# One unit's way through a cross-attention kernel, spread over three slots

## What is computed

```
res = x
h = _layer_norm(x, ln1_scale, ln1_offset)
x = res + _cross_attention(h, xf_1, wq1, bq1, wk1, bk1, wv1, bv1, wo1, bo1, bias_k1, bias_v1)
...
h = _layer_norm(x, ln_mlp_scale, ln_mlp_offset)
h = jax.nn.gelu(h @ w_fc1 + b_fc1, approximate=False) @ w_fc2 + b_fc2
return x + h
```

```
logits = jnp.einsum('bqhk,bthk->bhqt', qh, kh) / scale
weights = jax.nn.softmax(logits, axis=-1)
ctx = jnp.einsum('bhqt,bthk->bqhk', weights, vh).reshape(b, q_len, H * K)
return ctx @ wo + bo
```

## Time and profile before

| what | us |
|---|---|
| median of 3 runs | 1518.13 |
| the three runs | 1518.45, 1424.64, 1518.13 |
| the profiled execution, whole | 1426.43 |
| its span, first to last instruction | 1424.7 |
| PE busy in it | 1366.2 |
| DVE, ACT, POOL busy in it | 902.9, 620.4, 307.6 |

### The profile page before, as it was taken

The page is one execution under the profiler, slowest core; times in us unless marked ns, Lnnn a source line. Parts: engine busy times, 40 slices in busy tenths (PEclk is TensorE's granted clock), DMA queues, the critical chain, the costliest instruction groups (busy, mean ns, idle before and its releaser), DMA issues. The chain is left out here.

```text
span 1424.7 us, 27588 instructions
## 1 busy us (share of the span) xinstructions
PE 1366.2 (96%) x11607; PEld 1219.9 (86%) x11607; DVE 902.9 (63%) x1876; ACT 620.4 (44%) x1022; POOL 307.6 (22%) x290
## 2 busy tenths in 40 slices
PE   5999999999999999999999999998898999997898
PEld 4889998999999898999999999987887877776787
DVE  4866667576666777666666666668534378886322
ACT  4633433434343564334343434346422337775421
POOL 2201011010110112011011010112863023334654
PEclk9999999999999999999999999999999999998999
DMA  5100000001100000000000000000000000002000
GB/s 154 60 31 1 30 11 21 30 1 31 30 2 31 1 31 1 30 31 1 30 1 31 31 2 30 10 22 23 1 1 9 0 2 2 2 3 64 5 30 29
DMA packets 28012, 30.53 MB, mean 21 GB/s; under 512 B 684, under 2 KB 26868, under 8 KB 27892
## 3 DMA queue, kind: packets, MB, share of 16 engines
q1 hardware_dynamic: 27668, 28.72, 6.3%
q10 hardware_dynamic: 226, 0.10, 0.0%
HBM read 26.73 MB, written 2.10 MB: 20 GB/s over the span
## 5 line engine op out<-in xcount | busy, mean ns | idle before, releaser
L334 POOL TENSOR_TENSOR WLO<-W,WHI 128x512 fp32r<-128x512 f32 x64 | 80.7, 1290 | 765.9 <-DVE WHI L728 765.9
L761 DVE STREAM_TRANSPOSE PRT<-PR 32x256 f32<-32x256 f32 x512 | 223.2, 436 | 8.4
L768 DVE TENSOR_TENSOR CLO<-bank,CHI 128x512 fp32r<-128x512 f32 x128 | 88.0, 691 | 145.6 <-ACT CHI L649 145.6
L626 ACT ACTIVATE KT<-bank,PH 128x512 f32<-128x512 f32 x128 | 88.0, 688 | 186.1 <-PE bank L171 186.1
L169 PE MATMUL bank<-WHI,CHI 128*128 128x256 f32 x576 | 167.5, 291 | 0.0
L170 PE MATMUL bank<-WLO,CHI 128*128 128x256 f32 x576 | 161.5, 280 | 0.0
L171 PE MATMUL bank<-WHI,CLO 128*128 128x256 f32 x576 | 161.0, 280 | 0.0
L169 PE MATMUL bank<-WHI,SRC_HI 128*128 128x256 f32 x504 | 146.2, 290 | 0.0
L170 PE MATMUL bank<-WLO,SRC_HI 128*128 128x256 f32 x504 | 140.9, 280 | 0.0
L171 PE MATMUL bank<-WHI,SRC_LO 128*128 128x256 f32 x504 | 140.8, 279 | 0.0
L791 DVE TENSOR_TENSOR X<-X,bank 128x512 f32<-128x512 f32 x128 | 88.0, 688 | 68.0 <-PE bank L171 67.4
(11 more groups left out here) (230 smaller groups left out, 3124.2 us busy)
## 6 DMA issues: line engine op xcount, KB each, us to landing
W<-in_wall SPq DMA_DIRECT2D x17, 1024.0 KB, 5.6
W<-in_ctx SPq DMA_DIRECT2D x4, 512.0 KB, 6.8
X<-in_x SPq DMA_DIRECT2D x4, 512.0 KB, 8.6
mlp_w<-in_w SPq DMA_DIRECT2D x2, 1024.0 KB, 9.1
out<-X SPq DMA_DIRECT2D x4, 512.0 KB, 2.9
W<-in_wall SPq DMA_DIRECT2D x1, 512.0 KB, 6.5
W<-in_wall SPq DMA_DIRECT2D x2, 256.0 KB, 8.3
W<-in_qw SPq DMA_DIRECT2D x1, 256.0 KB, 2.8
```

What stands on the lines that cost most here:

```text
L334: i = e.tensor_tensor(WLO[a][:, j, :, :], W[a][:, j, :, :], WHI[a][:, j, :, :].bitcast(F32), ALU.subtract)
L626: e.activation(KT[:, h, :, 0:S], PROJ[2 + h][:, :].rearrange("p (q k) -> p q k", k=S), ACT.Identity, bias=PH[:, 1, 2 * pair + h:2 * pair + ...
L761: i = e.transpose(PRT[b * S + z:b * S + z + 32, :, b * S + y:b * S + y + 32], PR[b * S + y:b * S + y + 32, :, z:z + 32])
L768: e.tensor_tensor(CLO[:, h, :], bank[3 + h][:, :], CHI[:, h, :].bitcast(F32), ALU.subtract).then_inc(c_lo, 1)
```

## The change

A unit now takes three slots. In slot n PE runs keys(n), output(n-2), queries(n), values(n,0), values(n,1), scores(n), weighted(n-1). Its work is the same; `output` goes one slot back and stands behind the keys, and `weighted` goes from between the two halves of the values to the slot's end. ACT and DVE are rewritten to match: `exponential(n-1)` opens slot n behind `weighted_out(n-2)`, and of a LayerNorm the four `scale_chunk` steps of a group are done at the start of the slot behind its transpose. The bias transposes go through the logits banks (`TB`) in place of the projection banks. The tail is written anew: eight `up` blocks in place of four are placed ahead of the first `down`, with the last two units' steps between them, and the rounding of the MLP's second weights goes behind the last softmax. The core of the diff:

```diff
                     for n in range(1, SLOTS):
                         keys(n)
+                        if last_turn:
+                            e.wait_ge(sub_done, n)
+                            norm_turn(e, norm, NL, 0, TB)
+                        if n == 2:
+
+                            weighted(0)
+                        elif n > 2:
+                            output(n - 2)
...
                         queries(n)
                         values(n, 0)
                         if bias is not None:
-                            e.wait_ge(q_out, 2 * n + 2)
-                            bias_turns(*bias, PROJ, n - 1)
-                        weighted(n - 1)
+                            if last_turn:
+                                e.wait_ge(norm.scaled, (NL * G + 1) * DC)
+                            else:
+                                e.wait_ge(sub_done, n)
+                            bias_turns(*bias, (TB[1], TB[0]), n - 1)
+                        if n == 2:
+                            output(0)
                         values(n, 1)
...
                         scores(n)
-                        output(n - 1)
+                        if n > 1:
+                            weighted(n - 1)
...
-                    for q in range(4):
-                        up(q)
+                    up(0)
+                    up(1)
+                    output(SLOTS - 2)
+                    up(2)
+                    up(3)
                     e.wait_ge(sub_done, SLOTS)
                     bias_turns(NL - 1, G - 1, (TB[1], None), SLOTS - 1)
                     weighted(SLOTS - 1)
+                    up(4)
                     e.wait_ge(ptb_out, NL * G)
                     norm_turn(e, norm, NL, 1, TB)
+                    up(5)
                     output(SLOTS - 1)
-                    e.wait_ge(fc2_lo, 1)
+                    up(6)
+                    up(7)
                     e.wait_ge(norm.scaled, (NL * G + 2) * DC)
                     norm_turn(e, norm, NL, 2, TB)
-                    for q in range(4, MQ + 4):
+                    e.wait_ge(fc2_lo, 1)
+                    for q in range(4):
+                        down(q)
+                    e.wait_ge(norm.scaled, (NL * G + 3) * DC)
+                    norm_turn(e, norm, NL, 3, TB)
+                    for q in range(8, MQ + 4):
                         if q < MQ:
                             up(q)
...
@@ scalar
                     queries_out(0)
-                    for c in range(DC):
-                        scale_chunk(e, 0, 1, c, PROJ)
-                    exponential(0)
                     ctx_round(2)
                     norm_sqrt(e, norm, 0, 2)
                     for n in range(1, SLOTS):
+                        if n > 2:
+                            weighted_out(n - 2)
+                        exponential(n - 1)
+                        if before is not None:
+                            for c in range(DC):
+                                scale_chunk(e, *before, c, PROJ)
                         keys_out(n)
...
@@ vector
+                        if n >= 2:
+                            weighted_rest(n - 2)
...
                         softmax(n - 1)
...
+                        if n >= 2:
+                            settle(n - 2)
...
-                        weighted_rest(n - 1)
...
                         shifted(n)
-                        settle(n - 1)
...
+                    weighted_rest(SLOTS - 2)
                     softmax(SLOTS - 1)
+
+                    e.wait_ge(w_in[1], 8 * SETS)
+                    e.wait_ge(v_done, 2 * SLOTS)
+                    e.tensor_copy(WHI[1][:, 0:3, :, :], W[1][:, 0:3, :, :]).then_inc(fc2_hi, 1)
+                    settle(SLOTS - 2)
+                    rounded(0)
+                    rounded(1)
```

More of the change, by code:

```diff
@@ L345, in _ @@
                                     ALU.subtract).then_inc(w_split, 1)
-                    for n in range(SLOTS + 1):
+                    for n in range(SLOTS):
                         pair, a, g = unit(n)
-                        if n < SLOTS and g == 2 and pair + 1 < NL * HP + 1:
+                        before = apply_at(n - 1)
+                        if before is not None:
+                            norm_lo(e, norm, *before)
+                        if apply_at(n) == (NL, 0):
+                            norm_lo(e, norm, NL, 0)
+                        if g == 2 and pair + 1 < NL * HP + 1:
                             split(pair + 1, 1 - a)
-                        if apply_at(n) is not None:
-                            norm_lo(e, norm, *apply_at(n))
                     e.wait_ge(fc2_hi, 1)
@@ L363, in _ @@
                         if q == 1:
+                            norm_lo(e, norm, NL, 1)
+                        if q == 3:
+                            norm_lo(e, norm, NL, 2)
                             e.wait_ge(fc2_hi, 2)
@@ L366, in _ @@
                                             ALU.subtract).then_inc(w_split, 1)
-                        if q in (2, 4):
-                            norm_lo(e, norm, NL, 2 + (q - 2) // 2)
+                        if q == 7:
+                            norm_lo(e, norm, NL, 3)
                         if j == 5:
@@ L675, in _ @@
                             ctx_round(3)
+                        if n == 2:
+                            weighted_out(0)
+                        if apply_at(n) == (NL, 0):
+                            for c in range(DC):
+                                scale_chunk(e, NL, 0, c, TB)
                         queries_out(n)
@@ L678, in _ @@
                         if bias is not None:
-                            bias_out(*bias, PROJ[0])
-                        weighted_out(n - 1)
+                            bias_out(*bias, TB[1])
                         values_out(n, 1)
-                        if now is not None and now[0] == NL:
-                            for c in range(DC):
-                                scale_chunk(e, *now, c, PROJ)
-                        elif now is not None:
-                            scale_chunk(e, *now, 0, PROJ)
                         if took is not None:
                             norm_sqrt(e, norm, *took)
-                        exponential(n)
-                        if now is not None and now[0] < NL:
-                            scale_chunk(e, *now, 1, PROJ)
                     def gelu(q):
@@ L709, in _ @@
                         scale_chunk(e, NL, 1, c, TB)
+                    gelu(5)
                     for c in range(DC):
```

87 lines of the change are left out of this document (42 added, 45 removed).

## The result

| | median, us | runs |
|---|---|---|
| changed | 1514.8 | 1514.64, 1514.75, 1514.85, 1516.07 |
| before, beside it | 1472.61 | 1424.64, 1427.08, 1518.13, 1518.45 |

The kernel before has two kinds of runs, near 1426 and near 1518; the changed one showed only the upper kind. Set against the lower runs of the kernel before its ratio is 1.0626 (95% interval 1.06 to 1.0651): slower by 6%. Against the two upper runs of the kernel before (1518.13 and 1518.45) the changed one is 3.5 us lower.

The account below looks back on a forecast made before the run. PE's own work was taken to bound the middle slots, leaving only the edges to gain. Terms 0 + 2 - 0.6 + 0.6 - 6.7 = -4.7 us gave 1421.7 from the profiled execution, 1513 at the median's level; range 1408 to 1525.

Parts of the forecast that it names:

- from the sum to the time: Whole kernel: -4.7 us on the profiled 1426.43 gives 1421.7; moved to the runs' median 1518.13 it gives 1513.
- The 0.04: Whole kernel: chance left for a comparison mixing the two run levels, which would read as 6% either way.
- The middle slots (0): 62 middle slots: PE's work only trades neighbours, so no gain or loss; range -12 to +6 us.
- rival 2: Middle slots: scores and weighted side by side save the edge, 12 us more; 1410 or 1501; chance 0.10.
- rival 3: Output behind keys: `CLO` becomes the slot's bound, 0.8 us a slot, 50 in all; 1476 or 1568; chance 0.03.
- rival 4: Middle slots: PE has hidden room another order opens; closed wholly, 80 us, giving 1346; chance 0.01.
- The first slots (+2): Slots 1 to 3: new waits of 4.0 and 2.0, old 2.84 and 1.05 gone; +2 us, bounds 0 to +5.
- The layer border (-0.6): Slots 34, 35: new wait 1.3 against 1.9 us of old waits; -0.6, bounds -1.9 and +2.
- Slot 63 (+0.6): First MLP group's transpose behind keys(63) needs `XN` after `CLO`: 3.2 us and a little against 2.8; +0.6.
- The tail (-6.7): Tail: of 9.7 us lost, POOL's split wait goes, 3 stays at the last transpose; -6.7, bounds 9.7 and 1.6.
- The slow `norm_apply`: Tail, chain behind the last output: 5.08 us while POOL was busy, against 1.38; could cost 3.7 more.
- The sum (-4.7): All terms: 0 + 2 - 0.6 + 0.6 - 6.7 = -4.7 us; likeliest case, chance 0.62.

Follow-up runs that it names:

- second profile: The changed kernel run again unaltered, on another chip: 1514.36, 1514.97, 1515.15 and one run of 1428.05 us.
- another version: Changed kernel with the second unit's scalings back ahead of the first exponential and 10, 3, 3 spare matmuls in the first latent steps: ratio 0.9962; profiled run 1425.82 us.

## Why the prediction came near in its number and was wrong in its verdict

**The step that failed** is the one from the sum to the time: "nothing in the trace ... tells why", and then the same -4.7 moved to the median's level. The level was taken as a thing that the runs bring along and that the change leaves alone. It is a property of one stage, whose time the sum put at nothing as untouched, and the change, far ahead of it, raised the share of runs in which that stage stays at half clock. In the profiled executions it took 225.64 us in place of 133.33. The trace did tell: the same kind of window as the earlier trace rows, laid over the latent attention, has 6.83 us at 0.50 just at the entrance and then 126.3 us at 1.00 (1165.74 to 1292.03). This stage at half the clock is what fits the 92 us between two runs, as the runs then showed. The forecast asked what bounds the parts that were touched, and never what bounds the rest. The 0.04 set aside for "a comparison that mixes the two levels" had the size (6%): the ratio does set upper runs against lower ones. But it took the mixing for chance, where the kernel before is high in 19 of 51 runs and the changed one in seven of eight.

**The nearness of 1513 to 1514.8 is luck.** 1513 is the upper level because two of the three runs shown happened to stand there; from the profiled execution's own level the forecast was 1421.7, and the one low run of the changed kernel took 1428.05.

**The middle slots (0):** 14.28 against 14.32, and no wait on PE. The small difference is real and steady: from slot 4 to slot 29 the changed kernel gains 0.85 us (84.00 to 446.81 against 83.54 to 447.20), and from slot 36 to slot 61 again 0.85 (563.37 to 926.18 against 563.57 to 927.23). So -1.7 in place of 0, a small part of what rival 2 named (0.2 a slot); rival 3 (`CLO` as the bound) and rival 4 did not come.

**The first slots (+2):** waits of 4.22, 1.56 and 0.70 against 4.0, 2.0 and none. The half-clock stretch was not "the same once": 38.52 to 45.35, twice as long as before. (In the second profile of the changed kernel it was 3.41.)

```profile
38.52:45.35 6.83, 5.75 (x15) 4.63 (x16) 6.63 (x22) 2.25 (x4) 0.98 (x1) 0.50 0.25 82
```

Slot 4 begins at 84.00 with one output (2.8) less done than before at 83.54 (the earlier trace rows has the block at 2.93): +3.3, within the bounds. Undoing it gave 3.2 back.

**The layer border (-0.6):** slot 34 waits 1.26 where 1.3 was worked out, slot 35 not at all, against 0.84 and 1.05. The waits were right and the term was not: slots 29 to 35 together take 116.56 us (446.81 to 563.37) against 116.37, so +0.2. PE's own work in them takes longer, 115.30 us against 114.48 busy, which the term left out.

**Slot 63 (+0.6):** the transpose waits 0.21. Mis-sized, and small. The two rows of PE's timeline:

```profile
539.34 0.47 PE L169 MATMUL pair<-SRC_HI,WHI 128*128 128x512 f32 x1 [1.26 <-issue]
...
961.23 1.06 PE L138 MATMUL logits<-ident,XN 128*128 128x128 f32 x8 [0.21 <-DVE XN L129]
```

**The tail (-6.7):** the split's wait went, and what is late next is a transpose, as was said, but the second group's (2.23) more than the last (0.75): 3.0 in all, against 3 expected. The sum is right and its place is wrong. The slow `norm_apply` that the prediction set beside POOL's work came at the second group (4.06 us, 988.54) and not at the last, which took 1.54. There was no half-clock stretch in this execution; in the second profile of the same kernel there was one of 3.41 (990.42 to 993.83), behind the same wait of 2.23.

**The sum (-4.7):** at the ninth `up` block the changed kernel is 4.1 us ahead: +3.3 for the first slots, -1.7 for the middle ones, +0.2 for the border, and -5.9 from slot 61 on, with slot 63 and the tail, where the one output owed is made up. So the sum is close because errors of one to two microseconds cancel. Of the 4.1 it loses 1.6 again before the latent attention, 0.78 of it in a wait for POOL's low part at 1013.41 that no term had. With the clock held in the latent attention in both kernels the medians differ by -4.4. So the reasoning on the parts that the change touches held in sum, and was worth 0.3%.

## What to carry to other kernels

When the runs of a kernel stand at two levels, look for a stage that is long enough to account for the distance at half clock; then ask of any change, however far ahead, whether it can touch that stage's beginning. Here it was a long stage of small matmuls behind an idle time of 2.7 us, and spare dense matmuls laid mostly into the idle time itself settled it (none high in ten runs) at next to no cost. Judge a new order of work only with that settled in both kernels.

## What the runs showed of the hardware

A stage of transposes, 17-column and 64-row matmuls, with PE busy for all 60 of 60 us in the records, ran at a granted clock of 0.50 to its end in one execution (228.69 us with what follows) and, but for its first 6.3 us, at 1.00 in another. Some microseconds in, it keeps its level; at the entrance small matmuls alone have seen the clock come back (four traces, after 6.83 us). 24 dense matmuls of 512 columns brought 1.00 back within the stage, 5.2 us after they began. Between the two levels the same stage differs by a factor of 1.76 (923 against 525 matmuls in 60 us), not 2.

Whether it came back went with less than 1 us (3.68 against 4.13 us from the last projection to the fall). With 3 spare matmuls (some 0.2 us each: seven take 1.80 in the row above, from first start to last end) ahead of the projections the changed kernel had no high run of four, where it had seven of eight, and the kernel before four of four, where it had 19 of 51.

An idle time of 2.2 us in the tail was followed by a fall in some executions and not in others: by 0.50 for 3.41 us in the changed kernel's second profile and for 10.24 in another version's (2.21), by none in its first (2.23).
